# Work moved to GpSimd and reordered in the first five slots of a chunked recurrent layer with an FFN

## The reference, cut to what matters

```python
pre = einsum('btd,df->btf', layernorm(x), W) + b          # 4 gates of 256
i = 10 * tanh((i_pre + input_bias) / 10); f = -softplus(f_pre)
o = sigmoid(o_pre); tz = tanh(z)
# scan over t, per feature
m_next = maximum(f + m, i)
i_s, f_s = exp(i - m_next), exp(f + m - m_next)
c = f_s * c + i_s * tz ;  n = f_s * n + i_s
h = o * (c / (n + 1e-6))
# then
x = x + h / rms(h) * scale
u = layernorm(x)
out = x + u + 0.5 * (silu((layernorm(u) * gamma + beta) @ w1 + b1) @ w2 + b2)
# w1 = (fc1_q - 128) * fc1_scales, w2 = (fc2_q - 128) * fc2_scales
```

## Time and profile before

| | |
|---|---|
| time of the kernel before, 3 runs | 320.06, 321.01, 321.54 us, median 321.01 |
| time of the profiled execution | 321.89 us |
| its span | 320.0 us |
| TensorE busy | 303.9 us |
| VectorE busy | 267.4 us |
| ScalarE busy | 229.7 us |
| GpSimd busy | 118.1 us |
| mean granted TensorE clock | 0.989 |

### The profile page before, as it was taken

The page is one execution under the profiler, slowest core; times in us unless marked ns, Lnnn a source line. Parts: engine busy times, 40 slices in busy tenths (PEclk is TensorE's granted clock), DMA queues, the critical chain, the costliest instruction groups (busy, mean ns, idle before and its releaser), DMA issues.

```text
span 320.0 us, 4813 instructions
## 1 busy us (share of the span) xinstructions
PE 303.9 (95%) x1760; PEld 263.8 (82%) x1760; DVE 267.4 (84%) x474; ACT 229.7 (72%) x372; POOL 118.1 (37%) x126
## 2 busy tenths in 40 slices
...
DMA packets 10951, 14.21 MB, mean 44 GB/s; under 512 B 688, under 2 KB 10160, under 8 KB 10672
## 3 DMA queue, kind: packets, MB, share of 16 engines
...
## 4 chain that ended last, share of the span: by engine, by line
PE 45%; DVE 20%; issue 14%; POOL 12%; ACT 6%; DMA 3%; POOLq 0%; DVEq 0%; SPq 0%
PE mm_ps L221 7%; PE mm_ps L219 7%; PE mm_ps L220 7%; PE z_ps L220 6%; PE z_ps L219 6%; PE z_ps L221 6%; POOL rows L1034 3%; DVE rec L672 2%; DVE g L729 2%; DMA rows<-x 2%; POOL rec L1001 2%; DVE rows L737 2%; POOL g L1019 2%; DVE bn L742 2%; DVE rec L687 2%
## 5 line engine op out<-in xcount | busy, mean ns | idle before, releaser
L219 PE MATMUL z_ps<-w_hi,y_hi 128*128 128x256 f32 x248 | 71.3, 288 | 1.4 <-issue 1.4
L220 PE MATMUL z_ps<-w_lo,y_hi 128*128 128x256 f32 x248 | 70.4, 284 | 0.0
L221 PE MATMUL z_ps<-w_hi,y_lo 128*128 128x256 f32 x248 | 70.4, 284 | 0.0
L765 DVE TENSOR_TENSOR y_lo<-y,y_hi 128x512 fp32r<-128x512 f32 x64 | 43.2, 687 | 12.2 <-ACT y_hi L504 11.7
L501 ACT ACTIVATE y<-mm_ps,b_all 128x512 f32<-128x512 f32 x60 | 41.3, 688 | 13.4 <-PE mm_ps L288 9.8
L219 PEld LDWEIGHTS z_ps<-w_hi,y_hi 128*128 128x128 f32 x248 | 47.5, 191 | 1.9 <-issue 1.8
L220 PEld LDWEIGHTS z_ps<-w_lo,y_hi 128*128 128x128 f32 x248 | 47.2, 190 | 0.1
L221 PEld LDWEIGHTS z_ps<-w_hi,y_lo 128*128 128x128 f32 x248 | 47.1, 190 | 0.0
L1005 POOL TENSOR_TENSOR rrms<-meansq,minus_half 128x4 f32<-128x4 f32 x8 | 9.0, 1122 | 96.5 <-DVE meansq L723 96.5
L219 PE MATMUL mm_ps<-gt_hi,w_hi 128*128 128x512 f32 x108 | 43.2, 400 | 0.0
L220 PE MATMUL mm_ps<-gt_lo,w_hi 128*128 128x512 f32 x108 | 42.8, 396 | 0.0
...
## 6 DMA issues: line engine op xcount, KB each, us to landing
...
rows<-x SPq DMA_DIRECT2D x7, 512.0 KB, 6.4
...
wg_raw<-w_gates SPq DMA_DIRECT2D x1, 512.0 KB, 5.5
wg_raw<-w_gates ACTq DMA_DIRECT2D x1, 512.0 KB, 5.8
...
```

The lines of the kernel that those rows point to most:

```text
L219: pe.matmul(dst, wh[w_at], ah[a_at], start=start, stop=False)
L220: pe.matmul(dst, wh[w_at], al[a_at], start=False, stop=False)
L221: return pe.matmul(dst, wl[w_at], ah[a_at], start=False, stop=stop)
L765: dve.tensor_tensor(y_lo[:, j], y[:, j % YBUFS], y_hi[:, j].bitcast(F32), ALU.subtract).then_inc(y_lo_done, 1)
```

## The change

Seven edits, all in chunk 0 to 5.

1. ScalarE: the first table is `exp_and_others`, so that the tanh of i and `exp_i(0)` share it and one load ahead of `exp_i(0)` goes. In slot 3 the two i tiles of chunk 3 are evicted under the silu table, and the load of the sigmoid table comes behind them.
2. i times z of chunk 0 is done by GpSimd in two halves, each as soon as its z tile is there; `denominators` waits for a half at a time.
3. Rounding of w1 (one half by VectorE, one by ScalarE before) and of w2 (ScalarE before) goes to GpSimd, in two casts of 128x1024 each. So does `x_normalised(2)`, four instructions. `w2_lo` is made in two halves, ahead of `h_scaled(1)`.
4. VectorE, chunk 0: `h(0)` comes before `x_low(2)`, and `o_times_c(0)` between `newton(0)` and `refined(0)`.
5. TensorE: `h_turned(0)` is one gate tile earlier; g of chunk 0 is turned row by row as it comes, between 5/8 and 3/8 of `shifted_bias`.
6. `ln1(4)` and `ln1(5)` move: 4 behind `ln2(1)`, 5 ahead of `maximum(3)`.
7. Slot 4: `g_high(2)` comes ahead of `x_normalised(5)` on ScalarE, `x_high(5)` ahead of `exp_i(4)`; on VectorE `g_low(2)` comes right behind `denominators(3)`, and `base_bias(1)` and `final(1, 0)` behind `x_low(5)`.

```diff
@@ tensor
-            gates(2, range(0, 2))
+            gates(2, range(0, 1))
             h_turned(0)
-            gates(2, range(2, GJ))
-            shifted_bias()
-            g_turned(0)
+            gates(2, range(1, GJ))
+            shifted_bias(range(0, 5))
+            g_turned_by_rows(0)
+            shifted_bias(range(5, KF))
@@ scalar
-            act.preload_act_table_set("sigmoid_and_others")
+            act.preload_act_table_set("exp_and_others")
...
-            act.preload_act_table_set("natural_log_exp_and_others")
             exp_i(0)
...
-            gates(0, range(4, 7))
-            act.wait_ge(w1_scaled, 1)
-            act.activation(w1_hi[:, 1], w1_f[:, 1], ACT.Copy).then_inc(w1_rounded, 1)
-            gates(0, range(7, GJ))
-            x_normalised(2)
+            gates(0, range(4, GJ))
...
-            act.wait_ge(w2_scaled, 1)
-            act.activation(w2_hi[:], w2_f, ACT.Copy).then_inc(w2_rounded, 1)
...
+                if t == 4:
+                    gates(t, range(GJ))
+                    g_high(t - 2)
+                    x_normalised(t + 1)
@@ vector
             def denominators(c, blocks):
                 s = c % 2
-                dve.wait_ge(iz_ready, at(c, 1, 1))
                 for k in blocks:
+                    dve.wait_ge(iz_ready, at(c, 2, k + 1))
...
-            dve.wait_ge(w1_scaled, 1)
-            dve.tensor_copy(w1_hi[:, 0], w1_f[:, 0]).then_inc(w1_rounded, 1)
...
             newton(0)
+            o_times_c(0)
             refined(0)
-            o_times_c(0)
+            h(0)
             x_low(2)
-            h(0)
...
-            ln1_sums(4)
             mean_square(1)
-            ln1_means(4)
+            for u in range(2):
+                dve.wait_ge(w2_rounded, u + 1)
+                dve.tensor_tensor(w2_lo[:, 4 * u:4 * u + 4], w2_f[:, 4 * u:4 * u + 4],
+                                  w2_hi[:, 4 * u:4 * u + 4].bitcast(F32), ALU.subtract).then_inc(w2_ready, 1)
             h_scaled(1)
...
             y_low(1, range(7, KF))
+            ln1(5)
             maximum(3, range(KD))
@@ gpsimd
+            def input_times_z_by_tiles(c):
+                r = rec[c % 2]
+                pool.wait_ge(i_ready, at(c, 1, 1))
+                for k in range(KD):
+                    pool.wait_ge(gate_done, at(c, 8, 5 + k))
+                    pool.tensor_tensor(r[:, 2, k], r[:, 2, k], r[:, 1, k], ALU.mult).then_inc(iz_ready, 1)
...
-            input_times_z(0)
+            input_times_z_by_tiles(0)
+            x_normalised(2)
+            pool.wait_ge(w1_scaled, 1)
+            for k in range(KD):
+                pool.tensor_copy(w1_hi[:, k], w1_f[:, k]).then_inc(w1_rounded, 1)
...
             ln1_root(3)
+            pool.wait_ge(w2_scaled, 1)
+            for u in range(2):
+                pool.tensor_copy(w2_hi[:, 4 * u:4 * u + 4], w2_f[:, 4 * u:4 * u + 4]).then_inc(w2_rounded, 1)
             rms_root(1)
-            ln1_root(4)
             ln2_root(1)
+            ln1_root(4)
```

More of the change, by code:

```diff
@@ L354, in h_turned, with shifted_bias @@
                     ins.then_inc(ht_ready, 1)
-            def shifted_bias():
-                pe.wait_ge(w1_scaled, 1)
-                pe.wait_ge(gate_done, at(1, 8, 6))
-                for j in range(KF):
+            def shifted_bias(tiles):
+                if tiles[0] == 0:
+                    pe.wait_ge(w1_scaled, 1)
+                    pe.wait_ge(gate_done, at(1, 8, 6))
+                for j in tiles:
                     for k in range(KD):
@@ L841, in _ @@
             denominators(1, range(KD))
+            divisor(1)
+            g_low(0)
             dve.wait_ge(beta_w1, 1)
@@ L844, in _ @@
                               ).then_inc(b1_ready, 1)
-            divisor(1)
-            g_low(0)
             numerators(1)
@@ L872, in _ @@
             ln2(1)
+            ln1(4)
             maximum(2, range(KD))
@@ L898, in _ @@
             y_low(1, range(7, KF))
+            ln1(5)
             maximum(3, range(KD))
             for t in range(4, CHUNKS - 1):
-                if t > 4:
-                    y_low(t - 3, range(6, KF))
-                ln1(t + 1)
-                denominators(t - 1, range(KD))
-                divisor(t - 1)
-                numerators(t - 1)
-                o_times_c(t - 1)
-                g_low(t - 2)
-                base_bias(t - 3)
-                newton(t - 1)
-                refined(t - 1)
-                final(t - 3, 0)
-                h(t - 1)
-                x_low(t + 1)
-                input_times_z(t)
+                if t == 4:
+                    denominators(t - 1, range(KD))
+                    g_low(t - 2)
+                    divisor(t - 1)
+                    numerators(t - 1)
+                    newton(t - 1)
+                    o_times_c(t - 1)
+                    refined(t - 1)
+                    h(t - 1)
+                    x_low(t + 1)
+                    base_bias(t - 3)
+                    final(t - 3, 0)
+                    input_times_z(t)
+                else:
+                    y_low(t - 3, range(6, KF))
+                    ln1(t + 1)
+                    denominators(t - 1, range(KD))
+                    divisor(t - 1)
+                    numerators(t - 1)
+                    o_times_c(t - 1)
+                    g_low(t - 2)
+                    base_bias(t - 3)
+                    newton(t - 1)
+                    refined(t - 1)
+                    final(t - 3, 0)
+                    h(t - 1)
+                    x_low(t + 1)
+                    input_times_z(t)
                 maximum(t, range(KD))
```

53 lines of the change are left out of this document (35 added, 18 removed).

## The result

The kernel after takes **324.86 us** (median of 4 runs, 324.57 to 326.32), the one before beside it 321.27 (4 runs). The ratio is 1.0114, 95% interval [1.0082, 1.0146]: slower by 3.6 us, where the prediction had no change, and 1.1 us above its range. The profiled execution of after took 324.57 us, its span is 322.7 against 320.0. So the two traces differ by 2.7 us of the 3.6. A few executions of some kernels took far longer than the others, 327 to 766 us; none of them is counted in any ratio, and the traces of e1 and e3, which are of such executions, are not read.

A forecast was written before the change was run, and what follows sets the result against it. TensorE and VectorE were taken as nearly full, VectorE deciding up to slot 4. Shifts of -0.65, -0.15, +1.9 and -0.8 gave +0.3, after slot 4 and clock +0.5: 321.5 us against the median, range 318.2 to 323.8.

The forecast's parts named there:

- What GpSimd's new work costs VectorE: Lead-in to slot 3: casts and x_normalised(2) on GpSimd delay VectorE by 1.9 us, practical upper end 4.2.
- The 0.3 for `x_normalised(2)`: Chunk 0's scans of denominators and numerators: four GpSimd rows beside them cost VectorE 0.3 us, out of 0 to 1.0.
- The 1.6 for the casts: Four GpSimd casts of w1 and w2 cost VectorE 0.4 us each, out of 0 to 1.1.
- the heavy rival: Each GpSimd cast gets ahead of a two-input VectorE instruction: 4.2 us instead of 1.9, time 323.8 us; chance 0.24.
- The +0.25 of VectorE: In the trace of before, a GpSimd row of 0.56 us makes VectorE's next instruction 1.47 us instead of 1.22.
- Clock, counted 0.8: Slot 4: TensorE, idle 2.7 us ahead of h(3)'s transposes, may fall to half clock; counted as 0.8 us lost.
- Slot 4: Wait for x(5) goes, VectorE waits 2.5 us for chunk 5's load, x_low(5) shifts +0.6 beyond +0.3; fc1(2) at -0.3.
- Lead-in's gains: VectorE up to slot 3: chunk 0's recurrence -0.65 us, new order -0.15, waits that go -0.8.
- Sum: VectorE +0.3 us at the end of slot 3; fc1(2) -0.3, plus 0.8 for the clock, gives +0.5.
- Light company: GpSimd's casts find gaps and cost VectorE nothing: 318.8 us, or 319.9 with a fall of the clock; chance 0.20.
- a hidden load: Slot 4: chunk 5's rows land before VectorE reaches ln1(5), so no wait and full clock: 318.2 us; chance 0.08.
- the rival had 1.1: x_normalised(2) on GpSimd holds TensorE at x_turned(2) some 1.1 us, hidden behind VectorE: still 321.5; no chance of its own.

The follow-up runs named there:

- e1: The kernel after with the casts of w1 and w2 and x_normalised(2) taken off GpSimd again, all else kept; ratio to before 1.0053.
- e3: The kernel after with the casts and x_normalised(2) taken off GpSimd and ln1(5) behind maximum(3) again; ratio to before 0.9921.
- e14: The kernel before with slot 4's new order and the casts of w1, w2 and x_normalised(2) on GpSimd, w2_lo in one piece; ratio to before 1.002.
- e4: The kernel after with twelve extra matmuls, results unused, in TensorE's wait ahead of the transposes of h(3); ratio to before 1.0098.
- e5: The kernel after with only the two casts of w2 back on ScalarE; ratio to before 1.0085.
- e13: The kernel before with slot 4's new order and ln1(5) ahead of maximum(3); ratio to before 1.0021.

## Why the prediction was wrong

- **The step that failed** is "What GpSimd's new work costs VectorE", its term of +1.9 us. It measured 3.7 in the trace of after (2.0 at w1 and 1.69 at w2). The time of e14 puts GpSimd's new work as a whole at 3.4, which holds more than VectorE's loss: also TensorE's wait ahead of fc2(0), 2.21 us there, and its half clock. The term was mis-sized, not misplaced. The 0.3 for `x_normalised(2)` was right, 0.13 at the numerators and 0.19 at `o_times_c`. The 1.6 for the casts was 3.25: I took 0.4 each, "because GpSimd mostly waits for VectorE", and 0.8 as the practical upper end, and each cast that got in cost 0.73 to 0.85. The argument leaned on the one row in which GpSimd lost against back-to-back scans; at the casts VectorE runs separate instructions, and there GpSimd got in four times of four in after. It can lose there too, as in e4 and e5. The result is the heavy rival, with its chance of 0.24: its mark was 3.0 us in all, and its places, 31 to 39 and 67 to 76 us, are where the long rows stand. Its time was 323.8.
- **One row read amiss.** The row of 0.56 us at 236.43 ended at 236.99, ahead of the VectorE row of 1.47 at 238.10. Beside that one stood the next of the same kind, on record for 1.52 us from 236.97. The +0.25 of VectorE stands, but the pair 0.56 and 0.25 are two different instructions.
- **The rule weighed there.** By the Trainium skill, SBUF — State Buffer, section Who interferes with whom, the two engines exclude each other by an exclusive lock, where VectorE has two SBUF inputs or is in a two-port mode. The rows agree on who is hit: `refined`, `h` and y_lo with two SBUF inputs, and y_hi, a cast with one, 0.42 alone and 1.26 here; x_low, which reads PSUM, is not, 1.29 beside the cast at 37.00. The price by full length is near the rows as well, if the length is that of the cast alone: 1.04 us in e5, against 0.73 to 0.85 paid by VectorE. The lengths on record in after, 1.44 to 2.04, would give too much, since they hold GpSimd's own wait. Given the prediction's 1.1 for a cast, the rule's way of counting was the better one: 0.3 + 4.4 = 4.7 against the measured 3.7, where the forecast had 1.9.
- **Clock, counted 0.8.** fc1(2, 0) was +1.4 and its successor +2.6, so the fall behind h(3) cost 1.2; e4, where the clock held there, gives 1.2 too. TensorE's wait was 3.1 instead of 2.7 us.
- **Slot 4** held. Wait for the load 2.46 (2.5 forecast); x_low(5) came 0.4 later than VectorE's shift (+0.6); no wait for x(5) nor ahead of fc2(0). Slot 4's own net, all of edit 7 with ln1(5) ahead, was forecast at +0.2 (-0.3 + 0.8, less the +0.3 from the lead-in), and e13 gives +0.7, -0.2 to +1.6.
- **Lead-in's gains** held: denominators(0) -0.80 (-0.65), ending at 27.41 (27.5), order -0.15 (-0.15), waits -0.7 (-0.8). The sum at the end of slot 3 was +2.1 instead of +0.3, all of it company.
- **Sum.** +0.3 to +2.1 on VectorE gives fc1(2) at +1.4 instead of -0.3; with 1.2 for the clock it is +2.6 against +0.5, and +2.7 at the end of the span. From the forecast's basis, 321.01 + 2.7 = 323.7; the measured median is another 1.1 above, which these traces don't show. The ratio's interval, 2.6 to 4.7 us, just holds the 2.7.
- **The other rivals.** Light company and a hidden load are ruled out by the rows. `x_normalised(2)` was not late for TensorE in after; in e4 and e5 it was, by 1.06 and 1.18 us where the rival had 1.1, and no run shows whether that reaches the end. The 319.9 for light company with a fall of the clock doesn't fit the sum's own 0.8, by which it is 318.8 + 0.8 = 319.6.
